# Splitting the sum over heads of a softmax between VectorE and TensorE, units 7 to 14 of an attention and mixture-of-experts kernel

## The reference

```python
x = x + xattn(layernorm(x), ctx, Wq, Wk, Wv, Wo)    # 16 batches of 256 queries, 64 keys, D = 128
#   q, k, v: 16 heads of 8
#   scores = einsum('bhqd,bhkd->bhqk', q, k) / sqrt(8)
#   attn   = softmax(scores, axis=1)                 # over the 16 heads
#   out    = einsum(attn, v) @ Wo.T
x = x + ffn(layernorm(x))                            # 2 shared experts + top 2 of 8 routed experts
```

## Time and profile before

| what | value |
|---|---|
| time, median of 3 runs (lowest, highest) | 393.11 us (391.81, 393.36) |
| profiled execution, own time | 391.42 us |
| its span, first to last instruction | 389.6 us |
| busy share: TensorE, VectorE, ScalarE, GpSimd | 82%, 72%, 68%, 67% |
| mean granted TensorE clock | 0.963 |
| `max_heads` (L926), `sum_heads` (L931) | 16 times each, 36.5 us and 36.4 us together |
| slots 8 to 15 (start of the maximum) | 83.12, 89.46, 96.68, 103.92, 110.18, 116.64, 123.63, 130.86 us |

### The profile page before, as it was taken

How to read it: one execution, slowest core, us unless ns; L and a number is a source line. 1 busy time by engine, 2 the same in 40 slices (tenths; PEclk the granted TensorE clock), 3 DMA queues, 4 the chain that set the end, 5 groups by cost and what they waited for, 6 DMA issues and landing times.

```text
span 389.6 us, 11521 instructions
## 1 busy us (share of the span) xinstructions
PE 317.9 (82%) x3972; PEld 256.0 (66%) x3973; DVE 282.3 (72%) x584; ACT 264.0 (68%) x498; POOL 260.4 (67%) x268
## 2 busy tenths in 40 slices
PE   5865788566675688999999989799999999999252
PEld 1562456344454457888888666698998989999251
DVE  3789899999999979926747365667676777666255
ACT  2887799488586747565355879477676766767755
POOL 6264688789888593777777775067777777777600
PEclk9999699899989999999999999999999999999857
DMA  7957334310000000111113711413332322231098
GB/s 250 340 147 272 100 104 133 100 55 2 3 3 0 2 3 0 43 55 49 56 53 103 120 49 42 111 49 100 81 89 77 89 82 74 76 98 49 2 357 291
DMA packets 29178, 36.14 MB, mean 93 GB/s; under 512 B 4932, under 2 KB 24007, under 8 KB 28624
## 3 DMA queue, kind: packets, MB, share of 16 engines
q1 hardware_dynamic: 24592, 27.13, 23.1%
q0 software_dynamic: 4544, 8.44, 7.0%
HBM read 21.74 MB, written 14.72 MB: 94 GB/s over the span
## 4 chain that ended last, share of the span: by engine, by line
issue 27%; PE 21%; DVE 21%; POOL 16%; DMA 7%; ACT 4%; POOLq 1%; SPq 1%; DVEq 0%; ACTq 0%
POOL results L515 11%; DVE Z L931 6%; PE banks L1476 5%; DVE Mx L926 4%; POOL gathered L497 4%; DMA qRep<-results 2%; PE banks L1460 2%; PE banks L1461 2%; PE banks L1462 2%; DMA gathered<-xs,slot 2%; DMA q_rows<-qRep 1%; DVE rZ L934 1%; PE banks L1344 1%; PE banks L1354 1%; DVE stats L902 1%
## 5 line engine op out<-in xcount | busy, mean ns | idle before, releaser
L515 POOL DMA_INDIRECT results<-E,qRep x78 | 86.2, 1105 | 42.1 <-issue 28.2
L497 POOL DMA_INDIRECT gathered<-xs,slot x64 | 64.7, 1011 | 25.3 <-issue 18.6
L1212 DVE TENSOR_TENSOR E<-hid,E 128x512 f16<-128x512 f32 x78 | 54.0, 692 | 36.2 <-ACT E L780 35.9
L443 POOL TENSOR_TENSOR E<-E,rZ 128x1024 f32<-128x1024 f32 x32 | 67.5, 2131 | 17.6 <-DVE rZ L934 17.6
L778 ACT ACTIVATE hid<-banks 128x512 f32<-128x512 f32 x78 | 47.0, 603 | 38.0 <-DVE E L1212 21.0
L1576 PE MATMUL banks<-wprojL,E 128*128 x312 | 54.6, 219 | 2.9 <-DVE E L1212 1.9
L1580 PE MATMUL banks<-wprojH,E 128*128 x312 | 54.3, 219 | 0.0
L1578 PE MATMUL banks<-wprojH,E 128*128 x312 | 54.3, 219 | 0.0
L639 ACT ACTIVATE E<-banks 128x1024 f32<-128x1024 f32 x32 | 33.1, 1094 | 21.2 <-PE banks L1344 21.2
L780 ACT ACTIVATE E<-banks 128x512 f16<-128x512 f32 x78 | 47.3, 606 | 0.0
L1562 PE MATMUL banks<-qRep,wfcH 128*128 128x256 f16 x156 | 42.6, 273 | 0.7 <-ACT E L780 0.5
(11 more groups left out here) (223 smaller groups left out, 828.7 us busy)
## 6 DMA issues: line engine op xcount, KB each, us to landing
qRep<-gathered SPq DMA_DIRECT2D x39, 129.0 KB, 2.2
qRep<-q_rows SPq DMA_DIRECT2D x32, 128.0 KB, 2.6
qRep<-results SPq DMA_DIRECT2D x8, 512.0 KB, 6.8
X<-in_x SPq DMA_DIRECT2D x4, 512.0 KB, 6.7
q_rows<-qRep SPq DMA_DIRECT2D x8, 256.0 KB, 2.1
out<-X SPq DMA_DIRECT2D x8, 256.0 KB, 3.7
results<-E,qRep POOLq DMA_INDIRECT x78
gathered<-spare SPq DMA_DIRECT2D x9, 129.0 KB, 4.5
```

What stands on the lines that cost most here:

```text
L443: g.tensor_tensor(heads, heads, rZ[:, k % 2, :].unsqueeze(1).unsqueeze(3).broadcast_to([P, HH // 2, P, 2]), ALU.mult).then_inc(attn_ready, 1)
L497: g.indirect_dma_start(out=gathered, out_offset=bass.IndirectOffsetOnAxis(ap=slot[:, k, i:i + 1], axis=0), in_=xs[:, i, :], in_offset=None ...
L515: g.indirect_dma_start(out=results, out_offset=bass.IndirectOffsetOnAxis(ap=xg[:, k, h, 2 * D:ROW].bitcast(I32), axis=0), in_=yg[:, k, h, ...
L1212: v.tensor_tensor(gL[:, j, 2 * c:2 * c + 2], hid[:, 2 * j + c].rearrange("p (c q) -> p c q", c=2), gH[:, j, 2 * c:2 * c + 2], ALU.subtract ...
```

## The change

The sum of the exponentials of units 7 to 14 is split. TensorE adds heads 0 to 7 (columns g = 0 to 3, both halves of the last axis) as eight fp32 products with the identity, accumulated in 128 columns of bank 5 that the output projection does not write. VectorE reduces the other eight heads (1024 columns) and adds TensorE's 128 columns to the result. `half_sum(u - 1)` and `project_out(u - 3)` now follow directly on `raw_scores(u)`, ahead of `ffn_transposes`. Units 0 to 6 and 15 keep the full reduction.

The new waits: `half_sum(u)` waits for the first exponential of its unit, for `add_attention(u - 3)` (which reads bank 5) and for the sum of unit u - 1 (which read the same 128 columns). VectorE's addition waits for its own reduction, for `half_sum` and for the projection of unit u - 2, since TensorE must not write bank 5 while VectorE reads it.

```diff
--- before.py
+++ after.py
@@ -57,6 +57,7 @@
 NGRP = P // GRP
 LATE = PAIRS // 2
 WHOLE = 5
+SUMMED = 7
 PE_PAIRS = (1, 4)
 HALVES = SHARED * WHOLE
 
@@ -205,6 +206,7 @@
         scores = banks[:, 0:4, :]
         o_ps = banks[:, 4, :]
         y_ps = banks[:, 5, :]
+        z_ps = banks[:, 5, 2 * P:3 * P]
         t2_ps = banks[:, 6:8, :]
         r_ps = banks[:, 6, :]
         rank_ps, tot_ps = (banks[:, 6, i * 256:i * 256 + 256].rearrange("p (e t) -> p e t", e=EXPERTS)
@@ -252,6 +254,7 @@
         h32_ready, hlo_ready, gh32_ready, ghlo_ready = (
             sem(n) for n in ("h32_ready", "hlo_ready", "gh32_ready", "ghlo_ready"))
         shared_high, shared_low = sem("shared_high"), sem("shared_low")
+        zsum_ready, zhalf_ready = sem("zsum_ready"), sem("zhalf_ready")
         member_ready, rank_ready, slot_ready, token2_ready, table_ready = (
             sem(n) for n in ("member_ready", "rank_ready", "slot_ready", "token2_ready", "table_ready"))
         scattered = [sem(f"scattered{i}") for i in range(QUARTERS)]
@@ -926,10 +929,19 @@
                 v.tensor_reduce(Mx[:, k % 2, :], scores.rearrange("p b (h q) -> p q (b h)", q=P),
                                 AX_X, ALU.max).then_inc(max_ready, 1)
 
-            def sum_heads(u, k):
+            def sum_heads(u, k, halved):
                 dve.wait_ge(exp_done, 2 * u + 2)
-                v.tensor_reduce(Z[:, k % 2, :], E[:, k].rearrange("p g q o -> p q g o"), AX_XY,
-                                ALU.add).then_inc(z_ready, 1)
+                if halved:
+                    z = Z[:, k % 2, :]
+                    v.tensor_reduce(z, E[:, k, QUARTER:HH].rearrange("p g q o -> p q g o"), AX_XY,
+                                    ALU.add).then_inc(zhalf_ready, 1)
+                    dve.wait_ge(zhalf_ready, u - SUMMED + 1)
+                    dve.wait_ge(zsum_ready, u - SUMMED + 1)
+                    dve.wait_ge(y_ready, u - 1)
+                    v.tensor_tensor(z, z, z_ps, ALU.add).then_inc(z_ready, 1)
+                else:
+                    v.tensor_reduce(Z[:, k % 2, :], E[:, k].rearrange("p g q o -> p q g o"), AX_XY,
+                                    ALU.add).then_inc(z_ready, 1)
                 dve.wait_ge(z_ready, u + 1)
                 v.reciprocal(rZ[:, k % 2, :], Z[:, k % 2, :]).then_inc(rz_ready, 1)
 
@@ -959,7 +971,7 @@
                     if not (first and k == 0):
                         if not (first and k < 3):
                             dve.wait_ge(attn_ready, 2 * u - 4)
-                        sum_heads(u - 1, (k - 1) % 4)
+                        sum_heads(u - 1, (k - 1) % 4, not (first or second))
                     if first and k or second and k < 3:
                         low_q(u + 1)
                     if not (first and k < 3):
@@ -973,7 +985,7 @@
             with dve.Fori(2, PAIRS // 2) as n:
                 four_units(n, False, False)
             dve.wait_ge(attn_ready, 2 * UNITS - 4)
-            sum_heads(UNITS - 1, 3)
+            sum_heads(UNITS - 1, 3, False)
 
             def late_low(pair, j):
 
@@ -1346,6 +1358,16 @@
                     if i % 2:
                         last.then_inc(s_ready, 1)
 
+            def half_sum(u, k):
+                pe.wait_ge(exp_done, 2 * u + 1)
+                pe.wait_ge(x_added, u - 2)
+                pe.wait_ge(z_ready, u)
+                for g in range(QUARTER):
+                    for odd in range(2):
+                        last = t.matmul(z_ps, ident[:], E[:, k, g, :, odd], start=(g == 0 and odd == 0),
+                                        stop=(g == QUARTER - 1 and odd == 1))
+                last.then_inc(zsum_ready, 1)
+
             def weighted_values(u, k, half):
                 pe.wait_ge(attn_ready, 2 * u + half + 1)
                 for odd in range(2):
@@ -1377,6 +1399,9 @@
                     if k % 2 == 0:
                         pe.wait_ge(q_loaded[2 * n + k // 2], 64)
                     raw_scores(u, k, 2 * n + k // 2, first and k == 0)
+                    if u > SUMMED:
+                        half_sum(u - 1, (k - 1) % 4)
+                        project_out(u - 3, (k - 3) % 4, False)
                     if u < PAIRS:
                         prologue_rest(u)
                     if first and k == 0:
@@ -1385,8 +1410,6 @@
                         pe.wait_ge(qlo_ready, PAIRS)
                     if k > 1 and inputs:
                         ffn_transposes(2 * n - 6 + k, n > 2 or k > 2)
-                    if u >= PAIRS:
-                        project_out(u - 3, (k - 3) % 4, False)
                     values = not (first and k < 2)
                     if values:
                         if k % 2 == 0:
```

## The result

| | before | after |
|---|---|---|
| median of 8 runs | 392.54 us (391.81 to 394.88) | 389.63 us (387.26 to 390.47) |
| profiled execution, its span | 391.42, 389.6 us | 387.26, 385.5 us |
| busy share: TensorE, VectorE, ScalarE, GpSimd | 82, 72, 68, 67% | 86, 71, 68, 68% |
| mean granted TensorE clock | 0.963 | 0.962 |

The ratio is 0.9915, with a 95% interval of 0.9889 to 0.9941: 3.3 us less (2.3 to 4.4). 2.0 had been forecast, and that the difference would most likely not be told from none; it can be told.

A forecast was written before the change was run, and what follows sets the result against it. VectorE was taken to bound slots k = 1, 2, 3, the score loop slot 12. Saving 0.58 us in 8 slots, limited by TensorE's loop and GpSimd, moves unit 15's subtraction by 2.0: 393.11 - 2.0 = 391.1 us, range 389.3 to 394.0.

The forecast's parts named there:

- The half sum: TensorE, between scores and subtraction: 16 records of 0.111 us, 1.8 us a unit, bounds 1.7 and 2.3.
- the prediction's estimate by it: TensorE's eight fp32 products by the skill's 81 ns and four passes: 2.6 us a unit, set aside for the trace's rows.
- The move of the projection: Output projection ahead of the transposes: their waits on ScalarE's copy vanish, lay under the maximum and were worth nothing.
- TensorE's loop: Attention slots: half sum, projection, transposes and 3.2 us to the next scores; 6.0 us for k = 0, 1, 6.45 for k = 2, 3.
- the fall in slot 12: TensorE's slowed clock in slot 12 costs some 0.65 us now; counted on not to recur.
- the end: Behind unit 15's subtraction: its 2.0 us gain passes through experts, routing, scatter and gather to the kernel's end.
- This chain: Behind the last exponentials: TensorE's products, router, weighted values, ScalarE's copies and Gelus; starts with unit 15's exponentials, moves by 2.0 us.
- GpSimd's 2.7 us of lead: End of attention: unit 14's reciprocal 2.7 us earlier lets GpSimd's last multiplications start earlier; said not to count in full.
- VectorE's saving: VectorE's sum in 8 slots: 1.22 + 0.2 + 0.28 = 1.70 us against 2.28, 0.58 us less each.
- the gap between them: VectorE, between reduction and addition: a semaphore and two waits on registers, 0.2 us.
- The stretch from the maximum of unit 8: Attention, to unit 15's subtraction: from 83.12 us, the subtraction at 131.2 against 133.18, 2.0 us gained.
- the sum for the attention: Slot-by-slot forecast: slots 9 to 14 of 6.6, 6.65, 5.95, 6.9, 6.4 and 6.65 us, unit 15's subtraction near 131.2.

The follow-up runs named there:

- e9: Kernel before with only the output projection of units 5 to 12 moved ahead of the transposes; ratio 1.0015 (0.9985 to 1.0045).
- e6: Changed kernel with four more identity products in each half sum, 12 instead of 8; ratio 1.0074 (1.0038 to 1.011).
- e2: Changed kernel, but VectorE still reduces all 16 heads and does not use TensorE's sum; median 476.93 us against 475.36 for the kernel before.
- e7: Changed kernel with TensorE summing four heads instead of eight and VectorE twelve; ratio to the kernel before 0.9988 (0.9954 to 1.0023).
- e8: Changed kernel with TensorE's heads chosen by slot: eight at k = 1, 2, six at k = 3, four at k = 0; ratio 0.9983 (0.9946 to 1.002).
- e12: Changed kernel with heads split by slot and the router's exponentials written to PSUM; ratio to the kernel before 0.9944 (0.9917 to 0.997).
- e5: Kernel before with the router's exponentials written to PSUM, so VectorE's addition of 1 reads them there; ratio 0.9941 (0.9894 to 0.9987).
- e3: Kernel before with the addition of 1 to the router's exponentials moved from VectorE to ScalarE; median 475.31 us against 475.36.
- e11: Kernel before with the router's exponentials in PSUM, run once more for the whole time; ratio 0.9994 (0.9969 to 1.0019).
- e10: Changed kernel again, nothing edited; ratio to the kernel before 0.9929 (0.9899 to 0.996).
- e4: Changed kernel with the addition of 1 to the router's exponentials moved from VectorE to ScalarE; median 474.27 us against 475.36 for the kernel before.

## Why the prediction came out as it did

**What held.** The half sum was costed at 1.8 us. The projection follows its start by 1.89 to 1.92 us between the products, by 1.81 between the weight loads; from the sum's start to the subtraction 2.81 us were measured (2.75 costed), 3.26 with the transposes (3.2). The reduction takes 1.210 us (1.22), the addition 0.289 (0.28). So the 16 records ran near the 0.111 us of the earlier trace rows, and not as the 81 ns of the Trainium skill (TensorE: Matmul & The Clock Gate, Back-to-back issue gap) would give: the prediction's estimate by it was 2.6 us, measured are 1.9. How the two records of a product are related to the four passes named there, no run here shows. The move of the projection is worth nothing (e9), and TensorE's loop sets the start of slot 12 as the sum had it, GpSimd that of slot 13; at 2.7 us a half sum the first of them turns the change into a loss (e6). The clock did not fall in slots 8 to 15 of any of the four profiles of the changed kernel, nor in e2, e6, e7, e8 and e12, where TensorE adds up heads too. In each of the five without that load it did, in four of them in slot 12 and in e5 in slot 14. What the fall in slot 12 had cost was put too high, though, at 0.65 us: without it that slot takes 6.12 (e5), 0.34 less than the 6.46 of before.

**What failed: the end.** "This chain starts with the exponentials of unit 15, so it moves by 2.0." For TensorE that is so (its first product with `wprojH` moved by 0.13 more). The picking of the experts moved by 0.9 more, as the rank product, from 17.75 to 16.82 us behind the subtraction, shows. The prediction had GpSimd's 2.7 us of lead and let it lapse, since the copies and Gelus of ScalarE pace the weighted values. It overlooked that VectorE's first step behind them was being held by GpSimd's last multiplications, which in the changed kernel start 2.6 us behind the subtraction of unit 15 and not 3.8: the row of 1.40 us for 256 columns, over four times the 0.32 it takes alone, was in the trace of before, and the prediction does not mention it. e5 takes the hold away in the kernel before and gets 0.76 of the 0.9 us.

**What was mis-sized: VectorE's saving.** 0.58 us a unit was costed, 0.75 was measured (2.31 to 1.56). The reduction and the addition were right; the gap between them, for a semaphore and waits on registers, was put at 0.2 and is 0.03 us, the same as that between any two dependent steps there. All three waits in it are against values computed in registers, not two. So slots 9, 13 and 10, 14 take 6.24, 6.22 and 6.47, 6.46 us instead of the 6.4 to 6.65 forecast.

**What was not seen: the spread.** The stretch from the maximum of unit 8 was forecast at 131.2 - 83.1 = 48.1 us, and the changed kernel took 47.9 to 48.3 in four profiles. But the 50.06 it was set against was one of the quicker executions with the attention of before (49.8 to 51.8 in five profiles). The table shows two cases, by whether the clock falls in slot 7, ahead of the change, which happens in kernels of both kinds. Where it doesn't fall, the attention of before takes 49.8 to 50.1 us and the changed one 48.2 to 48.3: 1.5 to 1.8 gained, a little less than forecast. Where it falls to 0.77, 51.1 (e9) against 47.9: 3.1 gained. Where it falls to 0.58, the attention of before takes 51.8 (e3, e11). No profile has the changed kernel there; e8, the change with another split, took 47.49, so that some 3.9 gained is an estimate. Slot 8 then takes 7.3 us instead of 6.3 in kernels of both kinds, so it is not part of these gains. Two windows of e11, slots 7 and 12, of a kernel with the attention of before, show a first part of the difference:

```profile
74.76:82.91 8.15, 5.84 (x77) 4.25 (x77) 6.93 (x11) 2.62 (x4) 6.68 (x17) 0.58 0.24 68
110.92:118.17 7.25, 5.96 (x77) 3.79 (x77) 5.70 (x5) 5.83 (x12) 6.30 (x5) 0.61 0.01 2
```

The fall to 0.58 in slot 7 there goes with one to 0.61 in slot 12, and the slot takes 7.25 us; at 0.77 in slot 7 (e9) it is 0.74 and 6.51, no worse than before (0.74 and 6.46). In the changed kernel slot 12 is at full clock either way. The second part is a hold as at the end. Slot 11 begins VectorE's seeds with a `tensor_scalar` of 8 columns. In e10, with no fall in slot 7:

```profile
101.66 4.23 POOL L446 TENSOR_TENSOR E<-E,rZ 128x1024 f32<-128x1024 f32 x2
...
104.28 1.64 DVE L919 TENSOR_SCALAR var<-mv 128x8 f32<-128x8 f32 x1
...
106.34 0.20 POOL L459 TENSOR_TENSOR newton<-rstd 128x8 f32<-128x8 f32 x1 [0.46 <-DVE rstd L924]
```

and in the profile after, with one:

```profile
100.26 4.22 POOL L446 TENSOR_TENSOR E<-E,rZ 128x1024 f32<-128x1024 f32 x2 [0.22 <-DVE rZ L946]
...
104.12 0.38 DVE L919 TENSOR_SCALAR var<-mv 128x8 f32<-128x8 f32 x1
...
104.94 0.20 POOL L459 TENSOR_TENSOR newton<-rstd 128x8 f32<-128x8 f32 x1 [0.46 <-DVE rstd L924]
```

In e10 the step is issued while GpSimd is in its second multiplication and takes 1.64 us instead of 0.38; the Newton steps start later, and slots 11 and 12 take 6.78 and 6.86 instead of 6.16 and 6.25 (e4 the same, and e12 with its own split). In the profile after GpSimd had started unit 9 1.4 us earlier (1.2 measured from the maximum of unit 11), with 0.2 us of idleness ahead of it where e10 has none, and the step was held for nothing to speak of. So without a fall the change makes VectorE early enough to run into GpSimd, and loses 1.2 us. This is read from the rows and by comparing executions; no run takes that hold away.

That the sum for the attention came out right to 0.2 us was luck. In e10 slots 9, 10, 13 and 14 took 0.9 us less than forecast, by the better saving. Slot 11 took 0.8 more, by the hold (6.78, forecast 5.95), and the subtraction of unit 15 followed its maximum by 2.85 instead of 2.55. In the profile after, slot 8 took 0.9 more and slot 12 0.65 less than forecast instead.

**Together** the attention gains 1.5 to 3.1 us by the case (3.9 by the estimate) and the end 0.9, so 2.4 to 4.0 (4.8); measured were 2.3 to 4.4. Of the 4.1 us between the two profiled spans 1.15 had nothing to do with the change. The measured 389.6 us lies inside the forecast's range of 389.3 to 394.0, and the gain is 3.3 us where 2.0 was forecast: 0.9 of the excess is the end, the rest lies in the saving and the spread of the attention. What decides into which case an execution falls, and what starts the fall in slot 7, was not tried.

## What to carry to other kernels

Look for rows whose length does not fit their shape, before asking what waits for what: here a VectorE `tensor_scalar` on SBUF that took over four times its usual time beside a GpSimd multiplication was a wait, and the same line stood in the same profile with its usual time. Freeing GpSimd earlier is then worth more than its own queue shows. When work is moved into an engine's idle time, write down the loop of that engine as well, with the price at which it becomes the bound; here 0.9 us more a unit reversed the sign (e6). And take the stretch of before from several executions if a clock fall lies in or ahead of it: five profiles of the same attention lay 2 us apart in 50.

## What was not expected of the hardware

- A VectorE `tensor_scalar` on SBUF (256 columns, or 8) lasted 0.89 to 1.69 us in eight cases beside a running GpSimd multiplication (the kernel before, e2, e7, e8, e9; e4, e10, e12) and about 0.32 or 0.38 otherwise, each time ending within some 0.2 us of the multiplication's end (and 1.0 us in slot 7 of every kernel, ending with GpSimd's splitting of weights); read from PSUM it took 0.42 beside the same multiplication (e5, e11). Reductions (2.28 and 1.21 us), reciprocals (0.95) and the addition of TensorE's sum from PSUM (0.29) were not lengthened.
- Waits on three semaphores between two dependent VectorE steps in a hardware loop, all against register values, cost no more than one such wait: 0.03 us.
- An idle stretch of 2.25 us on TensorE, in e4, was followed by a fall to a granted clock of 0.52, and some 1.6 us of the rank product's delay came with it.
- The same attention ran alike to 0.01 us a slot in two profiles whose whole times were 387 and 472 us; the part behind the first rank products was slower in all runs of the experiments. Why is open.
